# Two attention heads in the rows of TensorE's array, with two buffers of their operands filled straight from SBUF

## The reference

```python
scores = jnp.einsum('bhld,bhsd->bhls', qh, kh) * inv_sqrt_d + bias[None]   # bias = -slope[h] * |i - j|
attn = jax.nn.softmax(scores, axis=-1)
out = jnp.einsum('bhls,bhsd->bhld', attn, vh)
...
x = x + 0.5 * ffn(layernorm(x), w_gate, w_up, w_down)
x = x + attention(layernorm(x), Wq, Wk, Wv, Wo, bo)
x = x + 0.5 * ffn(layernorm(x), w_gate, w_up, w_down)
```

## Time and profile before

| | |
|---|---|
| median of 3 runs | 909.1 us (907.73 to 913.88) |
| the profiled execution | 908.08 us, span 906.2 us |
| matmuls, busy | 4672, 838.6 us (93% of the span) |
| VectorE, ScalarE, GpSimd busy | 73%, 58%, 47% |
| mean granted clock of TensorE | 0.982 |

### The profile page before, as it was taken

How to read it: one execution, slowest core, us unless ns; L and a number is a source line. 1 busy time by engine, 2 the same in 40 slices (tenths; PEclk the granted TensorE clock), 3 DMA queues, 4 the chain that set the end, 5 groups by cost and what they waited for, 6 DMA issues and landing times.

```text
span 906.2 us, 15941 instructions
## 1 busy us (share of the span) xinstructions
PE 838.6 (93%) x4672; PEld 575.0 (63%) x4672; DVE 661.3 (73%) x1359; ACT 526.6 (58%) x745; POOL 425.9 (47%) x486
## 2 busy tenths in 40 slices
PE   3899998869999999999999999999999998999988
PEld 2788887735555665665665665565564447888877
DVE  5799997577677677677677677677678716777774
ACT  5344433415668658758758758768766684344443
POOL 0444433422635645645645644644644465344443
PEclk9999999967999999999999999999999999999999
DMA  9220000175383482482482482482482000010001
GB/s 382 83 66 7 0 0 2 38 197 140 83 223 69 106 221 50 103 222 48 98 222 53 95 225 53 93 225 56 91 228 54 3 1 2 25 46 23 23 23 48
DMA packets 37032, 84.48 MB, mean 93 GB/s; under 512 B 3746, under 2 KB 4770, under 8 KB 36818
## 3 DMA queue, kind: packets, MB, share of 16 engines
q1 hardware_dynamic: 36482, 83.45, 34.5%
q10 hardware_dynamic: 512, 0.53, 0.2%
HBM read 45.68 MB, written 38.87 MB: 93 GB/s over the span
## 4 chain that ended last, share of the span: by engine, by line
PE 76%; DVE 10%; DMA 5%; issue 4%; ACT 3%; POOL 1%; ACTq 1%; DVEq 0%; SPq 0%
PE ps L983 70%; DVE row_max L896 4%; DMA q_aug<-max_row 3%; PE ps L1034 2%; PE ps L995 2%; PE ps L1039 2%; DVE hid L784 1%; DVE xn L731 1%; ACT gated L590 1%; PE ps L1044 1%; DMA k_aug<-parts_scratch 1%; ACT stage L634 1%; DMA parts_scratch<-parts 1%; DVE w_max L846 1%; PE ps L1020 1%
## 5 line engine op out<-in xcount | busy, mean ns | idle before, releaser
L896 DVE TENSOR_REDUCE row_max<-ps 128x1 f32<-128x512 f32 x512 | 341.4, 688 | 125.3 <-PE ps L983 123.6
L678 ACT ACTIVATE probs<-ps 128x1024 f32<-128x1024 f32 x256 | 252.4, 1022 | 99.1 <-PE ps L983 88.3
L555 POOL TENSOR_TENSOR probs<-probs,diag 128x256 f32<-128x256 f32 x256 | 187.1, 733 | 231.7 <-ACT probs L678 231.3
L983 PE MATMUL ps<-k_aug,q_aug 96*128 96x512 f32 x512 | 221.5, 458 | 14.1 <-DVE row_max L896 6.8
L488 POOL TENSOR_TENSOR hid_r<-hid,hid_r 128x512 fp32r<-128x512 f32 x96 | 124.1, 1296 | 179.9 <-ACT hid_r L584 179.6
L983 PE MATMUL ps<-xnt,wgu_r 128*128 128x512 f32 x768 | 183.3, 395 | 14.5 <-DVE hid L784 7.0
L983 PEld LDWEIGHTS ps<-k_aug,q_aug 96*128 96x128 f32 x512 | 95.6, 194 | 146.4 <-DVE row_max L896 124.0
L983 PEld LDWEIGHTS ps<-xnt,wgu_r 128*128 128x128 f32 x768 | 142.9, 189 | 49.9 <-DVE hid L784 11.2
L983 PE MATMUL ps<-q_aug,k_aug 98*128 98x512 f32 x512 | 159.3, 404 | 7.3 <-DMA q_aug<-max_row 7.3
L983 PE MATMUL ps<-probs,v_aug 128*32 128x512 f32 x1024 | 137.1, 608 | 0.8 <-POOL probs L555 0.8
L590 ACT ACTIVATE gated<-ps 128x512 f32<-128x512 f32 x96 | 57.4, 598 | 116.6 <-PE ps L983 116.6
(11 more groups left out here) (62 smaller groups left out, 676.5 us busy)
## 6 DMA issues: line engine op xcount, KB each, us to landing
parts_scratch<-parts SPq DMA_DIRECT2D x128, 256.0 KB, 5.8
q_aug<-parts_scratch SPq DMA_DIRECT2D x32, 512.0 KB, 4.8
k_aug<-parts_scratch SPq DMA_DIRECT2D x32, 512.0 KB, 6.6
x_sb<-x_in SPq DMA_DIRECT2D x8, 512.0 KB, 12.7
x_out<-x_sb SPq DMA_DIRECT2D x8, 512.0 KB, 2.6
wgu_i<-w_gate_up SPq DMA_DIRECT2D x2, 768.0 KB, 5.9
k_aug<-k_rows_scratch SPq DMA_DIRECT2D x1, 1088.0 KB
w_att<-w_att SPq DMA_DIRECT2D x1, 1024.0 KB, 11.0
```

The source lines that it names most:

```text
L555: nc.gpsimd.tensor_tensor(tile, tile, diag[:, n * QH + 2 * pair:n * QH + 2 * pair + 2, :], ALU.mult).then_inc(fixed, 1)
L678: nc.scalar.activation(probs[:, kt % 2, 2 * pair:2 * pair + 2, :], ps[:, at:at + 2, :], ACT.Exp).then_inc(exp_done, 1)
L896: nc.vector.reduce_max(row_max[:, quad % 2, u % TT, u // TT:u // TT + 1], max_bank(b, tile)[0], mybir.AxisListType.X).then_inc(s1_used, 1)
L983: return nc.tensor.matmul(out, lhs, rhs, start=start, stop=stop, **k)
```

## The change

- **Rows.** q's parts now take `TERMS` = 3 sets of 16 rows (the product of the two rests is dropped), the bias 12 rows (6 segments in place of 8, and slopes that are powers of two times a unit, so that they need no second part), the maximum 2: 62 rows. Of the two heads of a step, one lies in partitions 0 to 61 and the other in 64 to 125. The scores of a step are one matmul on each half, into two banks; tiles for the maxima alternate between the halves too and are given out in twos. For odd heads the unit of the slopes is taken out of q by a scale for each partition (`q_scale`) and put back by the scale of the exponential.
- **Buffers.** `q_aug` and `k_aug` are two each, used in turn by the sequences; `parts` is one.
- **DMAs.** `move_rows` copies the split parts into the rows, SBUF to SBUF: 24 DMAs a turn of 64 partitions by 2 KB. `move_max` does what ScalarE's queue did for the maxima. All of it is on SyncE's queue, in a written order.
- **Maxima.** `max_in` is transposed by one matmul in place of four; `max_row` is 32 partitions by 128.
- **Order.** `FILLS` and the weights are new. The fills `max1`, `max2`, `max3` and `max0_next` stand one step later (steps 6, 7, 6, 6 in place of 5, 6, 5, 5), `MAX_LEAD` is 24. TensorE's turns are written out eight times in place of a loop.

```diff
 NQ = H // QH
 STEPS = 2 * TT
-SEG = 64
-NSEG = L // SEG
-ROW_BIAS = 4 * D
-ROW_MAX = ROW_BIAS + 4 * NSEG
+NSEG = 6
+HALVES = (0, 43, 85)
+TERMS = 3
+ROW_BIAS = TERMS * D
+ROW_MAX = ROW_BIAS + 2 * NSEG
 ROWS = ROW_MAX + 2
-PUTS = 16 * 4
+GROUP = 64
+NP = H // 2
+CHUNKS = 2
+MOVES = 16 * 2 * TERMS
 DEQ = float(np.float32(1.0 / 127.0))
...
 FILLS = {
-    (0, 3): "heads3_prev", (0, 5): "max1", (0, 6): "xt0_next", (0, 7): "xt1_next",
-    (1, 1): "turn1_prev", (1, 2): "qk0_next", (1, 3): "qk1_next", (1, 5): "heads0", (1, 6): "max2",
-    (1, 7): "qk2_next",
-    (2, 1): "qk3_next", (2, 2): "v0_next", (2, 3): "heads1", (2, 5): "max3", (2, 6): "v1_next",
-    (2, 7): "out0_prev",
-    (3, 1): "out1_prev", (3, 3): "heads2", (3, 5): "max0_next", (3, 7): "turn0",
+    (0, 2): "xt0_next", (0, 3): "heads3_prev", (0, 4): "xt1_next", (0, 6): "max1", (0, 7): "qk0_next",
+    (1, 0): "qk1_next", (1, 2): "turn1_prev", (1, 4): "out0_prev", (1, 5): "heads0", (1, 7): "max2",
+    (2, 0): "qk2_next", (2, 2): "qk3_next", (2, 3): "heads1", (2, 4): "out1_prev", (2, 6): "max3",
+    (3, 0): "v0_next", (3, 3): "heads2", (3, 4): "v1_next", (3, 6): "max0_next", (3, 7): "turn0",
 }
 ALL_FILLS = list(FILLS.values())
 
-BANKS_BEFORE = {"qk0_next": 0, "qk1_next": 1, "qk2_next": 2, "qk3_next": 3, "v0_next": 4, "v1_next": 5, "max0_next": 7}
+BANKS_BEFORE = {"qk0_next": 0, "qk1_next": 1, "v0_next": 4, "v1_next": 5, "qk2_next": 2, "qk3_next": 3, "max0_next": 7}
 FILLS_BEFORE = list(BANKS_BEFORE)
...
-WEIGHT_SCORES, WEIGHT_VALUES = 2, 4.4
-LN_SHARE = 0.8
-WEIGHTS = {"heads": 2, "max": 2, "turn": 2, "xt": 2, "qk": 6, "v": 6, "out": 6}
+WEIGHT_SCORES, WEIGHT_VALUES = 0.6, 1.0
+WEIGHTS = {"heads": 0.6, "max": 0.2, "turn": 0.55, "xt": 0.55, "qk": 1.4, "v": 1.7, "out": 1.7}
 MAX_TILES = 2 * NQ * STEPS
-MAX_LEAD = 28
+MAX_LEAD = 24
...
+                until = 2 * int(MAX_TILES // 2 * done / whole + 1e-6)
...
+            def lay_rows(side):
+
+                for i in range(2):
+                    sp.dma_start(q_aug[side][i * GROUP + ROW_BIAS:i * GROUP + ROW_MAX, :, :].bitcast(F32), d_qrows[i]
+                                 ).then_inc(aug_in[side], 16)
+                    sp.dma_start(k_aug[side][i * GROUP + ROW_BIAS:i * GROUP + ROWS, :, :].bitcast(F32),
+                                 d_krows.rearrange("r (o t) -> r o t", o=1).to_broadcast([ROWS - ROW_BIAS, NP, L])
+                                 ).then_inc(aug_in[side], 16)
+
+            def move_rows(b, name):
+
+                seq, kind, part = fill_parts(b, name)
+                chunk, is_k = part // 2, part % 2
+                wait_done(sp, b, name)
+                pairs = slice(chunk * NP // CHUNKS, (chunk + 1) * NP // CHUNKS)
+                for i in range(2):
+                    for term, half in enumerate((0, 0, 1) if is_k else (0, 1, 0)):
+                        at = i * GROUP + term * D
+                        to = (k_aug if is_k else q_aug)[seq % 2][at:at + D, pairs, :].bitcast(F32)
+                        sp.dma_start(to.rearrange("p q t -> p (q t)"),
+                                     parts[i * GROUP:(i + 1) * GROUP, is_k, half, :].bitcast(F32)
+                                     ).then_inc(rows_moved[is_k], 16)
+
+            def move_max(b, name):
+
+                seq, kind, part = fill_parts(b, name)
+                sp.wait_ge(drained, fill_no(b, name) + 1)
+                for i in range(2):
+                    at = i * GROUP + ROW_MAX
+                    sp.dma_start(q_aug[seq % 2][at:at + 2, 2 * part:2 * part + 2, :].bitcast(F32).rearrange("o j (t p) -> o (j t) p", p=P),
+                                 max_row[i * 4 * TT:(i + 1) * 4 * TT, :].bitcast(F32)
+                                 ).then_inc(max_moved, 16)
+
+            lay_rows(0)
+            for part in range(2):
+                move_rows(-1, f"qk{part}_next")
+            sp.wait_ge(ffn[0]["y_used"], 2 * B)
+            for part in range(2, 4):
+                move_rows(-1, f"qk{part}_next")
+            lay_rows(1)
+            move_max(-1, "max0_next")
+
+            for b in range(B):
+                move_max(b, "max1")
+                if not last(b):
+                    wait(sp, st_done, b * (NQ * STEPS))
+                    for part in range(2):
+                        move_rows(b, f"qk{part}_next")
+                move_max(b, "max2")
+                move_max(b, "max3")
+                if not last(b):
+                    for part in range(2, 4):
+                        move_rows(b, f"qk{part}_next")
+                    move_max(b, "max0_next")
...
                     wait(act, max_moved, quad_no * (16 * 2))
-                    nc.scalar.copy(max_row[:, :], bank[0:2 * QH, :]).then_inc(drained, 1)
-
-                    act.wait_ge(drained, at + 1)
-                    for i in range(2):
-                        act.dma_start(q_aug[ROW_MAX + i:ROW_MAX + i + 1, part * QH:(part + 1) * QH, :].bitcast(F32),
-                                      max_row[i * QH:(i + 1) * QH, :].bitcast(F32)).then_inc(max_moved, 16)
-
+                    nc.scalar.copy(max_row[:, :], bank[0:2 * TT * QH, 0:P]).then_inc(drained, 1)
+
+            act.wait_ge(scale_in, 16)
...
                         pe.wait_ge(neg_ready, seq * NQ + part + 1)
-                    for t in tiles:
-                        ins = nc.tensor.transpose(bank[0:2 * QH, t * P:(t + 1) * P], max_in[:, t, :], eye[:])
+                    if halves[0] == 0:
+                        ins = nc.tensor.transpose(bank[0:2 * TT * QH, 0:P], max_in[:].rearrange("p i o j t -> p (i o j t)"), eye[:])
                 elif kind == "heads":
...
                     quad, u = (tile // (2 * STEPS)) % NQ, tile % (2 * STEPS)
                     seq = b + tile // MAX_TILES
-                    h, t = quad * QH + u // TT, u % TT
-                    if u == 0:
-                        pe.wait_ge(aug_done[quad], (seq + 1) * (16 * 2))
+                    pair, t, rows = 2 * quad + u // STEPS, (u % STEPS) // 2, u % 2 * GROUP
+                    if u == 0 and quad % 2 == 0:
+                        for moved in rows_moved:
+                            pe.wait_ge(moved, (seq * CHUNKS + quad // 2 + 1) * MOVES)
                     bank, back = max_bank(b, tile)
                     wait(pe, s1_used, b * MAX_TILES + tile + 1 - back)
-                    matmul(bank, q_aug[0:ROW_MAX, h, t * P:(t + 1) * P], k_aug[0:ROW_MAX, h, :],
-                           True, True).then_inc(s1_done, 1)
+                    matmul(bank, q_aug[seq % 2][rows:rows + ROW_MAX, pair, t * P:(t + 1) * P],
+                           k_aug[seq % 2][rows:rows + ROW_MAX, pair, :], True, True).then_inc(s1_done, 1)
 
             def weigh_values(quad_no, quad, kt, seq):
...
-                            h = n * QH + 2 * pair + i
-                            ins = matmul(ps[:, scores_at + 2 * pair + i, :], k_aug[0:ROWS, h, kt * P:(kt + 1) * P],
-                                         q_aug[0:ROWS, h, :], True, True)
+                            rows = slice(i * GROUP, i * GROUP + ROWS)
+                            ins = matmul(ps[:, scores_at + 2 * pair + i, :],
+                                         k_aug[b % 2][rows, 2 * n + pair, kt * P:(kt + 1) * P],
+                                         q_aug[b % 2][rows, 2 * n + pair, :], True, True)
                         ins.then_inc(st_done, 1)
                         name = FILLS.get((n, s))
                         for piece, count in zip(pieces(n, s), TILES_AT[n, s]):
...
-            turns(pe, turn)
+            for b in range(B):
+                turn(b)
```

213 lines of the change are left out of this document (88 added, 125 removed).

## The result

The changed kernel takes 996.8 us (median of four runs, 994.3 to 1002.6) and the kernel before, on the same chip, 911.2. The ratio is 1.094, with a 95% interval of 1.090 to 1.098. The forecast was 870 and its range ended at 915: the prediction is wrong in sign and by 127 us. The profiled execution of the kernel after is the slowest of its four (1002.6), that of the kernel before one of the faster ones (908.1), so their spans lie 94.6 us apart where the medians lie 85.6.

The account below looks back on a forecast made before the run. TensorE's stream bounds the kernel. A turn becomes 52.5 (stream) + 9.2 (maximum stalls) + 2.0 (other waits) = 63.7 us; 31.5 off turns 0 to 6, 2 off turn 7, 5 ahead: 38.5 off 908.1, so 870 us, range 825 to 915.

Parts of the forecast that it names:

- What bounds the kernel before: Attention turns before the change: TensorE's stream fills 63.4 of 68.2 us; the 4.8 left are waits, mostly for VectorE.
- The pair: Scores and tiles: two matmuls on different row halves run side by side, 0.24 us a pair.
- The rival of halves in series: Scores and tiles: the second half waits for the first, 0.46 us a pair, 953 us in all; chance 0.11.
- The changes of form: TensorE's stream: 49 changes of array form a turn outside the values, at 0.09 us each, make 4.4 us.
- the prediction's sign (0.33): What would show the changes' cost: 0.33 us from a scores pair to a fill's first matmul.
- a full drain: Alternative price in TensorE's stream: each change of form costs 0.17 us, so 49 cost 8.3 us a turn.
- All 64 pairs as pairs: Scores and tiles of a turn: 64 pairs cost 15.4 us in place of 29.4.
- The maximum's way: Each quad's first scores wait for the maximum: stalls of 9.2 us a turn in place of 1.0.
- Other waits: Attention turns: TensorE's remaining waits, chiefly for VectorE through two banks, take 2.0 us a turn (0 to 6).
- The clock: Rival: TensorE loses its clock behind stalls, or changes cost more: 4 us more a turn, about 898; chance 0.12.
- Ahead of turn 0: Before the first turn: direct row moves, half the bytes and four tiles fewer take 5 us off (0 to 9).
- SyncE: DMA queue: row copies make max2 0 to 3 us late; rival, every maximum late, some 912 us, chance 0.07.

Follow-up runs that it names:

- e11: Kernel before, each maximum over 256 of its 512 keys, halving VectorE's reductions (leaves work out): 902.9 us, ratio 0.990.
- e4: Kernel after, with matmuls added where TensorE waits ahead of quads 0, 2, 3 and the fill xt0: 977.4 us, ratio 1.070.
- e5: e3 with tiles reordered so that two in a row use the same half of the rows: 1038.3 us, ratio 1.138.
- e13: Kernel before, scores over 62 rows and tiles over 60, as half-row matmuls without pairs (leaves rows out): 999.9 us, ratio 1.091.
- e7: e6 with e2's edit, 24 tiles ahead, and VectorE's rows for the next xt ahead of its reductions: 936.6 us, ratio 1.025.
- e10: e7 with each maximum over 256 of its 512 keys, halving VectorE's reductions (leaves work out): 903.1 us, ratio 0.990.
- e6: e3 with each step's two maximum tiles right behind its scores, for fewer changes of form: 957.6 us, ratio 1.047.
- e9: e7 with one maximum tile ahead of the step's scores and one behind them: 939.5 us, ratio 1.030.
- e12: e3, tiles still spread by weight, with e7's two edits on waits: 940.3 us, ratio 1.030.
- e15: e7 with tile pairs placed by hand, five in quad 0 in place of eight, 28 tiles ahead: 936.9 us, ratio 1.030.
- e2: Kernel after, with TensorE waiting for sequence 1's rows only ahead of their first tile: 984.2 us, ratio 1.077.
- e3: Kernel after, with each of the four maxima one step earlier and 28 tiles ahead: 961.9 us, ratio 1.053.
- e14: Kernel before, with max2 moved to (1,5) and heads0 to (1,6): 909.6 us, ratio 0.998.

## Why the prediction was wrong, step by step

Four terms of the sum failed, and the runs put a number on each: the stream's 52.5 us (4.4 for the changes of form, pairs that all close), the other waits' 2.0, the clock at nothing, and the 5 us off ahead of turn 0. The mechanism that the sum rested on, two matmuls side by side, came out.

**What bounds the kernel before: right, and closer than said.** TensorE's stream, said to be 63.4 of 68.2 us, with waits for VectorE as the rest. e11 took 15 us of VectorE's work away and won 0.3: the stream is about 66.4. So of the 4.8 us "mostly for VectorE" some 3 were not waits but distances that the sum had too short; one that the trace shows is the second matmul behind the values, 0.34 behind the first in place of 0.23 where both are tiles.

**The pair: right.** 0.24 forecast, 0.238 measured (e4). The rival of halves in series, the one case of the other side, was wrong as a mechanism; e5 shows what it would have cost, 3.3 us a turn for the tiles alone. That this rival's 953 lies nearer to the measured time than 870 is luck.

**The changes of form: a term that was mis-sized.** 49 changes at 0.09 made 4.4 us. e13 measures 0.17 each (9.2 / 55), for both sides of a change and the late second matmul together. The distances between starts say where it sits: 0.43 from a lone pair to the first product of qk in place of 0.23, the second product 0.34 behind the first, 0.33 back to a pair. Behind two pairs in a row the fill starts at 0.32, which is the prediction's sign (0.33); the late second pair it did not have. I had read only the way in and out of the values, with four column groups on either side, and missed that the matmul behind the first is late as well. At 0.17 it is 8.3, at the 0.20 of the distances 9.8: 4 to 5 us a turn. This is the 8.3 that the prediction worked out for a full drain and put aside. The Trainium skill's sentence (TensorEngine Tiling (Array Packing), Key Properties) that a change of tiling mode drains the engine had been the better guide; it gives no price, and e13's 0.17 agrees with a full drain as the prediction sized it.

**All 64 pairs as pairs: wrong.** In the turn from 614.9 to 689.9, 22 of the 64 tiles start apart from their partner, since VectorE hands the two banks back one by one, a reduction of 0.69 us each. An estimate from the distances between starts, at full clock: scores and tiles together take about 24 us (31 before), not 15.4, and all other work but the values about 18, not 15.3. With some 16 for the values the stream is 57 to 58 us, not 52.5. (The estimate takes a low value, near the tenth percentile, for each kind of distance, so it holds little of the late second matmuls; it moves by several us with the value taken.)

**The maximum's way: right in kind, too dear.** 9.2 us of stalls forecast, 4.6 measured in that turn; the longest at quad 2 (2.2, forecast 3.2). The likely reason, not tested, is that the forecast laid TensorE's work ahead of a quad too short, by the same missing changes.

**Other waits: too low, and the wrong ones.** 2.0 forecast. The wait for `xn` at xt0 (2.7, has none) stands at the fill that the change moved from (0,6) to (0,2), which the prediction did not cost; no run moves it back alone. In turn 7 the same fill waits for the second FFN's layernorm, and there it is one wait of 5.1 us (764.9 to 832.7; 687.3 to 743.1 of the kernel before has none), on top of 4.1 for the maxima:

```profile
PE ps L1022 <- DVE xn L743: 5.1, 1, 5.1
```

VectorE's loop through two banks holds 3.5 us or more (e7 against e10) that no spacing of the tiles took away (e6, e9, e12, e15).

**The clock: a rival, given 0.12.** Its mechanism came in, at a higher price (4 us a turn there) and together with the changes of form, which it had only as an alternative. I read in the earlier trace rows that a stretch with TensorE busy 2.54 of 4 us, 692 to 696, was "at the full clock still", and took it that few stalls would lose it. The row ends 0.15 us too early. The very next stretch of the kernel before is at half clock, with TensorE busy throughout:

```profile
696.20:699.60 3.40, 3.40 (x12) 1.16 (x4) 3.14 (x7) 0.65 (x2) 0.54 (x1) 0.51 0.02 5
```

So the trace of before already showed that stalls this short lose the clock. The profiled kernel after had 51 us at half clock ahead of turn 0 and within it (27 before) and one to four shorter stretches in each turn. An upper bound of its price, length times what is missing from 1.00, is 42 us over turns 0 to 6 (1 before) and 12 in turn 7 (2 before). e4 gives back 22 us with added matmuls alone, so a good part of it is real. The Trainium skill's rule (TensorE: Matmul & The Clock Gate, Part 1), that an idle engine goes back to its lower clock, agrees with e4's 0.98 to 1.00 in place of 0.89 to 0.95; that the engine can stay there without being idle is e13's.

**Ahead of turn 0: overlooked.** -5 forecast, +20.3 measured. The prediction noted that `lay_rows(1)` stands ahead of `move_max` in the queue, and not that TensorE's own wait asks for both sides. e2 puts 15 us on it. Nor did the 5 us come in without it: in e2 the first exponential is at 213.7, 1.4 later than before.

**SyncE: right on the maxima, not on the copies.** Its queue held no maximum up: each of the 32 is issued within 0.03 us of the end of ScalarE's copy. At quad 2 ScalarE's copy ends at 649.81 and the first DMA is issued at once (order of time, kernel after); the scores start at 652.5, 2.7 us later, forecast 3.2:

```profile
649.57 0.24 ACT L667 CAST max_row<-ps 32x128 fp32r<-32x128 f32 x1
649.83 0.65 SPq L454 DMA_DIRECT2D q_aug<-max_row  x1
```

The row copies land later than the prediction allowed. It called itself wrong if they took over 5 us, and those of k do, by their median over the whole kernel (page, part 6):

```profile
q_aug<-parts SPq DMA_DIRECT2D x96, 128.0 KB, 4.5
k_aug<-parts SPq DMA_DIRECT2D x96, 128.0 KB, 6.2
```

In the turns no matmul waits for them (235 to 740); ahead of turn 0 they are the 7.7 us of e2.

**The sum.** Against the forecast's 38.5 off stand 94.6 on, 133 us apart: 25 ahead of turn 0, 89 in turns 0 to 6 (12.7 a turn), 14 in turn 7, 5 behind. Of the 12.7, the runs support about 5 for the stream, up to 6 for the clock, 2.7 for `xn` and 3.5 for VectorE's loop against the 2.0 that the forecast had for both, less 4.6 for the maxima: some 10 to 11. They overlap and don't add up exactly. e3, e6 and e7 together take back 63 of the 85 us that the change costs (ratio 1.094 to 1.025). What stays open is why e10's turn is still 65.3 us, and what brings the clock back.

No version of the changed kernel that does all the work beats the one before: at full clock e7's turn is 68.8 us against 68.1, with 63 us of TensorE busy in place of 67. e14 is even with it.
